# Gated cross-attention and feed-forward on one core: seven products for eight in the last half of gate and up

## What is computed

```python
# attention part: 4 heads of 128, Wh per head; k = v = context
masked = scores(xn @ Wh, ctx @ Wh) * Dn
A = jnp.maximum(jnp.abs(masked.sum(axis=0)), 1.0)      # summed over all 64 sequences
O = einsum('hst,bthe->bshe', A, V)
Y = (O - mu) / jnp.sqrt(var + 0.001) * gn_gamma + gn_beta
x = x + tanh(g_xattn) * ((relu(xn @ wg_w) * Y) @ wo_w)
# feed-forward part: 512 -> 1408 -> 512, xn2 = layernorm(x), weights are -1, 0 or 1
g = (xn2 @ gate_w.T) * gate_s
u = (xn2 @ up_w.T) * up_s
x = x + tanh(g_ffn) * ((silu(g) * u) @ down_w.T * down_s)
```

## Time and profile before

| what | us |
|---|---|
| median of 3 runs | 1615.54 |
| lowest, highest | 1614.23, 1616.17 |
| the profiled execution | 1615.26 |
| its span, first to last instruction | 1613.5 |
| PE busy in it | 1549.4 |
| DVE, ACT, POOL busy | 995.9, 477.0, 663.6 |

### The profile page before, as it was taken

The page is one execution under the profiler, slowest core; times in us unless marked ns, Lnnn a source line. Parts: engine busy times, 40 slices in busy tenths (PEclk is TensorE's granted clock), DMA queues, the critical chain, the costliest instruction groups (busy, mean ns, idle before and its releaser), DMA issues.

```text
span 1613.5 us, 20040 instructions
## 1 busy us (share of the span) xinstructions
PE 1549.4 (96%) x7402; PEld 1296.8 (80%) x7402; DVE 995.9 (62%) x1492; ACT 477.0 (30%) x723; POOL 663.6 (41%) x749
## 2 busy tenths in 40 slices
PE   6999999998999989999998999999999999999999
PEld 5888888887777878777787877778888888888887
DVE  7677777768887878788797878864232233233222
ACT  3444444442312223131222313222322322322321
POOL 4555455523645546264454635532312311311311
PEclk9999999999999999999999999999999999999999
DMA  7787777765667667667775766763231231231220
GB/s 242 267 273 269 261 243 253 236 216 189 172 177 222 163 200 202 174 179 182 210 178 186 190 201 178 188 183 92 53 79 27 53 79 27 53 78 29 51 66 27
DMA packets 349635, 255.97 MB, mean 159 GB/s; under 512 B 258464, under 2 KB 259616, under 8 KB 349344
## 3 DMA queue, kind: packets, MB, share of 16 engines
q1 hardware_dynamic: 349536, 254.67, 53.3%
HBM read 156.05 MB, written 107.22 MB: 163 GB/s over the span
## 4 chain that ended last, share of the span: by engine, by line
PE 87%; DVE 7%; POOL 2%; issue 2%; DMA 2%; ACT 1%; SPq 0%; DVEq 0%
PE ps L1173 54%; PE pyb L1073 15%; PE ps L1108 5%; PE po L1073 5%; PE ptb L1073 5%; PE ptb L1078 2%; DVE xn L758 1%; DVE raw L728 1%; POOL reg L1003 1%; DMA wy_scratch<-misc 1%; POOL reg L1011 1%; DVE misc L725 1%; DVE reg L773 1%; DVE tmp L779 0%; DVE xbuf L769 0%
## 5 line engine op out<-in xcount | busy, mean ns | idle before, releaser
L1011 POOL TENSOR_TENSOR reg<-tmp,reg 128x512 fp32r<-128x512 f32 x176 | 237.0, 1347 | 563.8 <-ACT reg L527 562.9
L1173 PE MATMUL ps<-reg,gate 128*128 128x512 f32 x1408 | 357.9, 397 | 24.3 <-DVE reg L773 24.3
L1173 PE MATMUL ps<-reg,up 128*128 128x512 f32 x1408 | 351.8, 392 | 0.0
L779 DVE SCALAR_TENSOR_TENSOR tmp<-ps,colsb,tmp 128x512 f32<-128x512 f32 x176 | 131.2, 746 | 327.4 <-PE ps L1173 325.9
L1173 PEld LDWEIGHTS ps<-reg,gate 128*128 128x128 f32 x1408 | 267.3, 191 | 82.2 <-DVE reg L773 27.3
L1173 PE MATMUL ps<-xreg,reg 128*128 128x512 f32 x1408 | 324.2, 389 | 0.0
L1173 PEld LDWEIGHTS ps<-reg,up 128*128 128x128 f32 x1408 | 268.3, 191 | 56.7
L1173 PEld LDWEIGHTS ps<-xreg,reg 128*128 128x128 f32 x1408 | 263.8, 188 | 54.5
L537 ACT ACTIVATE tmp<-ps,colsb 128x512 f32<-128x512 f32 x176 | 121.4, 689 | 358.1 <-PE ps L1173 358.0
L527 ACT CAST reg<-tmp 128x512 fp32r<-128x512 f32 x176 | 109.3, 621 | 360.4 <-DVE tmp L779 360.3
L975 POOL TENSOR_SCALAR rs<-mv 128x1 f32<-128x1 f32 x192 | 48.1, 251 | 343.2 <-DVE mv L639 152.2
(11 more groups left out here) (103 smaller groups left out, 1615.8 us busy)
## 6 DMA issues: line engine op xcount, KB each, us to landing
xr<-in_x SPq DMA_DIRECT2D x63, 512.0 KB, 5.2
raw<-in_ctx_t SPq DMA_DIRECT2D x32, 512.0 KB, 4.7
w_scratch<-tmp SPq DMA_DIRECT2D x64, 256.0 KB, 4.0
v_scratch<-tmp SPq DMA_DIRECT2D x64, 256.0 KB, 3.8
raw<-v_scratch SPq DMA_DIRECT2D x32, 512.0 KB, 4.9
raw<-w_scratch SPq DMA_DIRECT2D x64, 256.0 KB, 4.1
x_scratch<-xr SPq DMA_DIRECT2D x32, 512.0 KB, 5.1
xr<-x_scratch SPq DMA_DIRECT2D x32, 512.0 KB, 4.9
```

The costliest lines, as they stand in the source:

```text
L779: e.scalar_tensor_tensor(tmp[:, m % 3, :], banks[2 * (n % 2) + 1], colsb[:, NI + j:NI + j + 1], tmp[:, m % 3, :], ALU.mult, ALU.mult).then ...
L1011: e.tensor_tensor(hid[1][:, m % 11, :], tmp[:, m % 3, :], f(hid[0][:, m % 11, :]), ALU.subtract).then_inc(s["hlo"])
L1173: last = e.matmul(dst, l, r, start=(k == 0 and i == 0), stop=(k == n - 1 and i == 1))
```

## The change

Groups 0 to 7 (NS = 8) are computed as before. Groups 8 to 15 are taken in NP = 4 pairs m of two groups, a and b, and gate and up of a block are one 2x2 block product: weights [[G1, G2], [U1, U2]] over the halves of the 512 inputs, tokens [[A1, B1], [A2, B2]]. Seven products (P1 = G1 A1, P2 = G2 A2, P3 = S4 B2, P4 = U2 T4, P5 = S1 T1, P6 = S2 T2, P7 = S3 T3) with sums S of weights and T of tokens give the four results in place of eight. Each is two input tiles times high and low part: 28 matmuls for a block of 1024 tokens (`seven`), where up_mm had 2 x 16. The parts that go with it:

- POOL makes the weight sums in groups 9 to 12 of the first stage (weight_sums), SP stores them at the head of groups 10 to 13 (sums_store), DVE looks for their low bits (low_sums). The mask is now one step that ors into lowacc, in place of a mask and a reduction. In group 0 of the middle stage SP copies G1, G2 and U2 (weights_copy). The seven weight blocks of a j, 7 KB a partition, are streamed with three buffers (weights_in).
- Of each pair of groups SP loads four x2 pairs (pair_in), DVE makes the sums T in place (combine), ACT and DVE split the seven operands (operand_hi, operand_lo), in the four downs of group 7 and the first four slots of each pair's eight downs.
- Copies of P1 and P5 (ACT), p15 (POOL), u2, c12, c22, c21 and hidden_a, hidden_b (DVE) put the results together.
- Hidden is kept whole (`hall`) and split tile by tile in two buffers (`hsp`): split_hi on ACT, split_lo on POOL, 128x1408 each. down_mm becomes down_of, in the banks ptb and pyb.
- Pairs of tiles start every 3.5 steps (first_step). v_load, v_hi and v_pair_lo come a piece earlier; x2_pair_lo stands directly behind the output step of its slot.

```diff
 def first_step(q):
-    return 15 * (q - 3) // 4 + 1 if q > 2 else -2
+    return 7 * (q - 3) // 2 + 1 if q > 2 else -2
...
+                if n >= 3:
+                    p.wait_ge("p4", n - 2)
+                e.dma_start(f(wbuf[n % 3][:, :, :, :]), ws_s[n % NI]).then_inc(s[f"wq{n % 3}"], 16)
...
             for g in range(NG):
                 more = g + 1 < NG
+                if 10 <= g < 14:
+                    sums_store(g - 10)
...
+            for m in range(NP):
+                q = 2 * NS + 4 * m
+                for j in range(NI):
+                    n = NI * m + j
+                    if j == 3 and m + 1 < NP:
+                        for i in range(4):
+                            pair_in(q + 4 + i)
...
+                    if n and n + 2 < NI * NP:
+                        weights_in(n + 2)
...
+            for m in range(NP):
+                t = 4 * NS + 8 * m
+                finish(t - 1)
+                for j in range(NI):
+                    n = NI * m + j
+                    if j:
+                        c21(n - 1)
+                    u2(n)
+                    if j:
+                        hidden_a(n - 1)
+                    c12(n)
+                    c22(n)
+                    hidden_b(n)
+                c21(n)
+                hidden_a(n)
+                for i in range(7):
+                    if m + 1 < NP and i < 4:
+                        prepare(m + 1, i)
+                    finish(t + i)
...
+                p.wait_ge("sadd", 4 * u + 1)
+                e.tensor_tensor(to[1], to[0], g1, ALU.subtract).then_inc(s["sadd"])
...
+            def p15(n):
+                p.wait_ge("p1c", n + 1)
+                p.wait_ge("p5c", n + 1)
+                e.tensor_tensor(p5b[n % 2][:, :], p5b[n % 2][:, :], p1b[n % 2][:, :], ALU.add).then_inc(s["p15"])
...
+                add(p1, G1, A1, 0, 2).then_inc(s["p1"])
...
+                add(p5, S1, T1, 0, 2).then_inc(s["p5"])
+                if j:
+                    p4(n - 1)
...
+                add(p6, S2, T2, 0, 2).then_inc(s["p6"])
+                p.wait_ge("p1c", n + 1)
+                add(p1, G2, A2, 2, 4).then_inc(s["p2"])
+                p.wait_ge("p5c", n + 1)
+                add(p5, S4, B2, 2, 4).then_inc(s["p3"])
+                p.wait_ge("u2", n + 1)
+                add(p6, S3, T3, 2, 4).then_inc(s["p7"])
+                if j == NI - 1:
+                    p4(n)
```

439 lines of the change are left out of this document (379 added, 60 removed), and 3 rows, old and new, of the table SEMAPHORES.

## The result

The changed kernel took **1655.7 us** (1654.9 to 1657.2), the kernel before 1615.1: a ratio of **1.0252** with a 95% interval of 1.0235 to 1.027, so 41 us slower where 7.5 were forecast. The profiled run's span is 1652.4 us against 1613.5, 38.9 us more.

The account below looks back on a forecast made before the run. TensorE was taken to set the time at both ends, with holes in the middle stage. 1615.3 - 39.9 - 44 + 26 + 11.6 + 11 + 1 + 42 = 1623 us, range 1588 to 1656.

Parts of the forecast that it names:

- Part 1, seven products: Gate and up of the last eight groups: 176 matmuls saved on PE, 39.9 us, all counting if PE never waits.
- Part 2, the middle stage: Groups 0 to 7: earlier x2 and V low parts and denser pairs close PE's waits, -44 us (-20 to -53).
- Part 3, the weight sums: First stage, groups 10 to 13: POOL's sums and their store delay V's stores and copies, +26 us (8 to 32).
- Parts 4 and 5, the costs of the pair stage: Last eight groups: waits within product sets and in the downs, 11.6 + 11 + 1 + 42 us.
- stream of weights: Pair stage: sixteen block loads ahead at j = 3 make weights 3 to 5 us late, three times, +11 us (0 to 16).
- downs: Eight downs of each of three pairs: operand preparation and DVE/POOL exclusion delay hidden splits, +42 us (6 to 48).
- c22 wait: Each pair's last P4 waits for c22, with DVE's multiply held behind POOL's split: 2.9 us, four times, +11.6.
- lone 1: The last pair's downs: cast, low part and gaps take 5.1 us against 5.0 per down, +1 us.
- The fourth in the list: Middle stage: DVE becomes the bound, gain 12 us instead of 44, total 1655 us; chance 0.17, slower.
- The second (sums hidden): First stage: sums' store waits little and V's store lands in time, cost only 4 us, total 1601; chance 0.20.
- the third (no exclusion that matters): Pair stage: DVE and POOL hardly block each other, downs cost 6 us and c22 4, total 1579; chance 0.10.
- The fifth (weights late in every set): Pair stage: streamed weights starve PE in every product set, 2 us x 44, total over 1700; chance 0.03.

Follow-up runs that it names:

- combo2: Changed kernel: sums stored later, POOL's sums halved, next pair's block loads and preparation spread, DVE's combinations one down earlier, x2's parts at old place in group 0; 1601.5 us.
- x2_back: Kernel before with the denser pace (3.5 steps) and V's chain moved earlier, x2's high and low parts left at their old places; 1575.6 us, ratio 0.9756.
- sums_later: Changed kernel with the store of the weight sums issued behind the group's third V store, not at the group's head; 1638.7 us, ratio 1.0134.
- blocks_spread: Changed kernel with the next pair's sixteen block loads issued four by four behind the weights, not all at j = 3 ahead of them; 1633.6 us, ratio 1.0109.
- changed_x2_back: Changed kernel with x2's high and low parts back at their old places behind the pieces of their step; 1639.5 us, ratio 1.0141.
- pace_back: Changed kernel with a piece every 3.67 steps of the middle stage, not every 3.5; 1662.7 us, ratio 1.0294.

## Why the prediction was wrong, step by step

**Part 1, seven products: -39.9.** It stands as PE work: the last two windows have 180 fewer matmul records (1932 against 2112, 176 by count). Even with costs around it cut, only 8.4 us of it are left: the last eight groups take 470.3 us in combo2 where they took 478.7.

**Part 2, the middle stage: -44, measured -16.0. This is the step that failed.** It says: "The change puts this low part straight behind the output step of its slot: with the same cast at 566.1 it ends near 568, 4 us before the boundary." The cast's time was read at one boundary and kept for all, and only the low part's own end was followed. ACT had stood 11.82 us for the block loads even there: the queue of the earlier trace rows said that the data were just in time, so an instruction moved ahead of them makes DVE stand. DVE stood 43.1 us in eleven waits, 34 of them in five waits of 3.2 to 8.7 us, and that took back 16 to 20 us of the stage (729.4 against 713.1, 725.7 against 706.2). Not each standstill costs: the longest ends group 6, which loses 2.4 us, before a group 7 that loses nothing. The prediction asked what is late next behind the denser pairs, and not what stands behind the moved wait on its own engine. The other half of the step, V's chain and the pace, gives 39.2 us, close to the 44. So the 28 us that are missing are 16.3 for x2's place, 6.9 for what the rest of the change does in this stage (the cause stays open), and 4.8 between 44 and 39.2. The prediction also counted its 53 us of loss from 411.7 us on; 8.6 more lie in the 26.3 us of group 0 ahead of that (17.7 us of work), and even x2_back still loses 14.5 us in group 0, against 8.0 in all the others. But I had its cause wrong in part: I counted the denser pace as a cost and x2's place as the cure, and it is the pace that ends most of x2's stops.

**Part 3, the weight sums: +26, measured +29.4.** Right in mechanism and size: V stores of 7.1, 6.9, 6.9 and 6.4 us and ACT waiting for them, with the first V copy at 252.43 where the forecast had 254. sums_later cut 16.4 of it by the store's place alone; the last 12 to 13 were not reached by any run.

**Parts 4 and 5, the costs of the pair stage: 65.6, measured 65.4** (504.2 for the last eight groups, less 478.7 - 39.9). The sum is right by two errors that cancel. The *stream of weights* was given 11 and took **24.9** (the first three pairs of blocks_spread; 26.4 with the last pair's 1.6): three waits of 5.4 to 6.1 us, 17.1 in all, and behind each a stretch at the lower clock that the step left out. The *downs* were given 42 and took about **27**: pairs of 121.1, 121.9 and 122.0 us in blocks_spread against 112.8 for the last, which prepares nothing. The stop before the fourth down was there, for POOL's split behind ACT's late cast, but of 4.3 to 4.5 us and not 7, and 0.9 at the fifth where I had 2 to 3. The last pair there, 112.8 against 109.7 of work without a wait (11 x 28 + 8 x 22 matmuls), carries the c22 wait (2.2 us, where I had 2.9) and the lone 1: 3.1 four times is 12.4, where I had 12.6.

**The rivals.** The fourth in the list, DVE as the bound of the middle stage, named the measured time (1655) and nearly the size (12 instead of 44; 16.0 measured), but that is luck, since its mechanism is not what the runs show. DVE did not lack time, it stood: it is busy 596.4 us in the middle stage of the changed kernel and 597.5 in that of changed_x2_back, which is 16.3 us shorter. Had load been the cause, pace_back would have been faster; it is 7 us slower. The second (sums hidden) and the third (no exclusion that matters) fell with parts 3 and 5. The fifth (weights late in every set) fell too: there are three such waits, not 44. The measured time lies just inside the stated range, but the sum behind it missed by 33 us, so that is luck too.

## What to carry to other kernels

When an instruction is moved up in its engine's queue, find out when its input is there at every place where it runs, not at one; if the input is only just in time, the move turns one stop into a standstill of everything behind it. Where a stop comes back once a period, compare the periods of the interleaved loops before the order within one: 15/4 steps times four was just one group, and a pace of 3.5 was worth 24 us by itself. When a change moves work between groups, compare what each loses above its work, not its length. A large transfer is placed by who queues behind it: sixteen small loads spread over a few sets gave 22 us, and one store moved behind the group's third V store 17. A saving of work on the busiest engine is worth what its helpers leave: 39.9 us fewer matmuls came to 8 us in the best order tried, and the kernel without them stayed ahead.

## What the runs showed of the hardware

Issuing block loads on SP took about 1 us each (14 in 14.8 us from 1159.61; four in 3.24 us in the earlier trace rows), in the long row more than their 0.83 us of transfer worked out from the earlier trace rows. Three stops of PE of 5.4 to 6.1 us were each followed by a stretch at a granted clock of 0.60 to 0.68, with 18 to 21 matmuls in the time of 32; that made each weight wait nearly half as dear again (24.9 us for 17.1 of waits). A DVE instruction of 1.21 us took 4.2 beside POOL's split of 3.2 and ended behind it, and POOL's split was itself stretched to 4.16; both sides of such a meeting pay. Left open: what holds group 0 of the changed kernel at 102 us with x2 in its old place, where x2_back has 97.8; what of the rest of the change costs 7 us in the middle stage; and whether the last 12 us of the first stage can be had with the sums in another stage, which was not tried.
